# Two-layer attention and feed-forward kernel: the expert stage written out chunk by chunk in place of a loop over three chunks

## The chip, the cores and the metric

The kernel runs on one core of a Trainium2 chip. The metric is the device time of one execution in microseconds (us). The engines are TensorE (PE; its weight loads are shown apart as PEld), VectorE (DVE), ScalarE (ACT), GpSimd (POOL) and SyncE (SP, which here only issues DMA transfers). Each engine has its own stream of instructions, and the streams meet at semaphores.

## What is computed

Two layers work on 128 sequences of 64 tokens with 128 features. Each adds an attention over a context and a feed-forward part to the running x. The change touches only the feed-forward part of the first layer, a mixture of 64 experts (eight chosen for each token) and one shared expert:

```python
def _L0_ffn_ref(x, centroids, expert_biases, Ws_up, Ws_down, W_up, W_down):
    ...
    shared = jax.nn.silu(xf @ Ws_up) @ Ws_down
    aff = xf @ centroids.T
    biased = aff + expert_biases
    _, idx = jax.lax.top_k(biased, TOP_K)
    sel = jnp.take_along_axis(aff, idx, axis=1)
    w = jax.nn.sigmoid(sel)
    w = w / (jnp.sum(w, axis=-1, keepdims=True) + 1e-08)
    cw = jnp.zeros((T, E), dtype=x.dtype).at[jnp.arange(T)[:, None], idx].add(w)
    h = jax.nn.silu(jnp.einsum('td,edf->etf', xf, W_up))
    y = jnp.einsum('etf,efd->etd', h, W_down)
    routed = jnp.einsum('etd,te->td', y, cw)
    return (shared + routed).reshape(B, S, D)
...
    x = x + _L0_xattn_ref(_layernorm(x, axis=-1), ctx_1024, ctx_1024, ...)
    x = x + _L0_ffn_ref(_layernorm(x, axis=-1), ...)
    x = x + _L1_xattn_ref(_layernorm(x, axis=-1), ctx_1024, ctx_1024, ...)
    x = x + _L1_ffn_ref(_layernorm(x, axis=-1), ...)
```

## The kernel before

The kernel has four stages, each a block in which every engine has its own code and at whose end all engines meet: `attention`, `experts`, `tail` (second attention) and `ternary` (second feed-forward part). The change is inside `experts`, which takes the time from 320.9 us to some 1102 us of the profiled execution.

`experts` computes all 64 experts for all tokens and weighs each expert's result with a gate that is zero where the token did not choose it. The tokens come in 16 chunks of 512. The experts come in pairs, and the pairs in groups of two, so that a chunk has 17 turns: 16 full ones, and turn 16 (`FULL`) with the shared expert alone. A turn n goes through the engines in this order:

- PE, `up` (L1133 to L1135): three matmuls for each pair (the weights and the tokens are split in a high and a low part) into the buffer `pu`.
- ACT (L1099): SiLU in place. DVE (L1036): product with the gates, `m`. The gates come by DMA from `scratch` in memory (L994, issued by SP).
- ACT (L1109), one turn later: the high part `mh` of `m`. The low part `ml` is made by DVE (L1041) or, for the turns 4, 5, 7, 10, 14 and for 16 in half size, by POOL (L955, L952).
- PE, `down` (L1144, L1145, L1148), three turns later: the sum over experts in `py`. For turn 0 of a chunk it first waits until ACT has copied out the `py` of the chunk before (`y_copy`, L1086), which ACT does in turn 2.

Beside this each chunk has work that is tied to fixed turns i: the layer norm and the routing of the next chunks (in `ChunkNorm` and `Routing`), and the adding of the finished chunk to x. Three of these places matter here. In turn 10, DVE sums a chunk's eight gates (`add_up`, L805), adds the epsilon (`add_eps`, L809, four numbers for each partition) and inverts (L813); POOL's L955 for turn 10 comes at nearly the same time. In turns 11 and 12, DVE takes the statistics of chunk c + 2 (L638, L644). In turn 12, POOL waits for them and normalises (`norm`, L650 to L657), and behind that in POOL's queue stands L955 for turn 14, whose `ml` PE needs in turn 0 of the next chunk.

The order is written out by hand in one function `step(n, r, chunk)` for each engine. `drive` (L905) calls it for each turn: for chunk 0 with plain numbers; then in a hardware loop (`eng.Fori`, L911) whose body is three chunks long and runs four times, for chunks 1 to 12; then with plain numbers again for chunks 13 to 15. Three chunks are a period, because the rings of three buffers come round. In the loop body a turn's number is only known in a register, so the values that semaphores are waited for, and the places in x, are worked out by register instructions (L52, and L638 for the addresses). `wait_apart` (L55) also adds an instruction that counts up an idle semaphore where the value is in a register; with plain numbers it is a bare wait. `live`, `exists` and `first` leave out work at either end.

Of the kernel before, what the change touches and what calls it, by code (L numbers as in the profile page):

```python
# [54 lines left out]
def wait_apart(eng, sem, value, idle):  # L55

    at_least(eng, sem, value)
    if not isinstance(value, int):
        eng.sem_inc(idle, 1)
# [16 lines left out]
def live(t, lag, count):  # L76

    return not isinstance(t, int) or 0 <= t - lag < count
# [757 lines left out]
def experts(nc, cst, x_res, norms, routing, entry, y_mean, y_rstd, sem, chunks=TILES // 4):  # L836
# [7 lines left out]
    GROUPS = (PAIRS + 1) // 2  # L844
    FULL = GROUPS - 1
    turns = chunks * GROUPS
    looped = (chunks - 4) // 3 * 3
    RING = 3
    SPREAD = 4
    with ExitStack() as mem:  # L850
# [51 lines left out]
            else:  # L902
                at_least(eng, gated, c * FULL + i + 1)

        def drive(eng, step):  # L905

            for n in range(GROUPS):
                step(n, n, lambda lag, n=n: (n - lag) // GROUPS)  # L910
            with eng.Fori(0, looped // 3) as g:  # L911
                for r in range(3 * GROUPS):
                    step(g * (3 * GROUPS) + (GROUPS + r), GROUPS + r, lambda lag, g=g, r=r: g * 3 + (1 + (r - lag) // GROUPS))
            for n in range((1 + looped) * GROUPS, turns + RING):
                step(n, n % (3 * GROUPS), lambda lag, n=n: (n - lag) // GROUPS)

        def exists(c):
# [5 lines left out]
        with nc.Block() as block:  # L923
            @block.gpsimd
            def _(pool):
                pool.sem_inc(y_rooted, 2)

                def after(semaphore, value):
                    wait_apart(pool, semaphore, value, idle["pool"])

                def y_root(c):

                    after(y_stats, 2 * c + 2)
                    nc.gpsimd.tensor_scalar(y_ve[:], y_mv[:, :, 1:2], 1e-5, None, ALU.add).then_inc(y_eps, 1)
                    nc.gpsimd.tensor_tensor(y_mean[:, bass.ds(c * 4, 4)], y_mv[:, :, 0], cst["ones"][:, 0:4],
                                            ALU.mult).then_inc(y_rooted, 1)
                    after(y_eps, c + 1)
                    nc.gpsimd.tensor_tensor(y_rstd[:, bass.ds(c * 4, 4)], y_ve[:, :, 0], cst["mhalf"][:].to_broadcast([P, 4]),
                                            ALU.pow).then_inc(y_rooted, 1)

                def norm(c):
                    routing.await_turned(pool, c - 1)
                    norms.norm(pool, x_res, cst["mhalf"], c, idle["pool"])

                def step(n, r, chunk):
                    i = r % GROUPS
                    if live(n, 1, turns) and (r - 1) % GROUPS in low_by_pool:
                        k = (r - 1) % 3
                        after(m_high, n)
                        after(down_done, n - 3)  # L950
                        if (r - 1) % GROUPS == FULL:
                            nc.gpsimd.tensor_tensor(ml[k][:, 0, :], m[k][:, 0, :], mh[k][:, 0, :].bitcast(F32),  # L952
                                                    ALU.subtract).then_inc(m_low[1], 1)
                        else:
                            nc.gpsimd.tensor_tensor(flat(ml[k][:]), flat(m[k][:]), flat(mh[k][:]).bitcast(F32),  # L955
                                                    ALU.subtract).then_inc(m_low[1], 1)
                    if not live(n, 0, turns):
                        return
                    c, first = chunk(0), isinstance(n, int) and n < GROUPS
                    if exists(c + 1):  # L960
                        if i == 1:
                            routing.low_part(pool, c + 1, (r // GROUPS + 1) % 3)
                        if i == 2:
                            routing.ends(pool, nc.gpsimd, "pool", c + 1)
                        if i == 3:
                            routing.fourth_powers(pool, nc.gpsimd, "pool", c + 1)
                        if i == 4:
                            routing.denominator(pool, nc.gpsimd, "pool", c + 1)
                        if i == 9:
                            routing.weights(pool, nc.gpsimd, "pool", c + 1)  # L970
                        if i == 11:
                            routing.gates_of(pool, nc.gpsimd, "pool", c + 1)
                    if i == 9 and not first:
                        y_root(c - 1)
                    if i == 12 and exists(c + 2):
                        norm(c + 2)
                drive(pool, step)

            @block.sync
            def _(sp):  # L980
                def step(n, r, chunk):
                    if not live(n, 0, turns):
                        return
                    i, c = r % GROUPS, chunk(0)
                    if i == FULL:
                        if exists(c + 1):
                            routing.store(sp, c + 1, (r // GROUPS + 1) % 3)
                        return
                    if i == 0:
                        wait_apart(sp, stored, 16 * (c + 1), idle["sp"])  # L990
                    wait_apart(sp, gated, c * FULL + (i + 1 - SPREAD), idle["sp"])
                    rows = scratch[(r // GROUPS) % 3, 4 * i:4 * i + 4].rearrange("(j e) t -> e j t", e=2)
                    for e in range(2):
                        sp.dma_start(gt[i % SPREAD][64 * e:64 * e + 64], rows[e].unsqueeze(0).to_broadcast([FH, 2, 512])).then_inc(  # L994
                            spread[i % SPREAD], 16)
                drive(sp, step)
                for n in range(4):
                    entry.load(sp, n)
                sp.wait_ge(stored, 16 * chunks)

            @block.vector
            def _(dve):
# [25 lines left out]
                def step(n, r, chunk):  # L1028
# [43 lines left out]
                    if exists(c + 2):  # L1072
                        if i == 11:
                            stats_of(c + 2)
                        if i == 12:
                            aggregate(c + 2)
                drive(dve, step)
                dve.wait_ge(y_rooted, 4)
                for n in range(2):
                    entry.norm_in(x_res, y_mean, y_rstd, n)  # L1080
# [1 line left out]
            @block.scalar  # L1082
            def _(act):
                def y_copy(c):
                    at_least(act, down_done, (c + 1) * GROUPS)
                    nc.scalar.copy(yT, py[:]).then_inc(y_out, 1)  # L1086

                def step(n, r, chunk):
                    i, k = r % GROUPS, r % 3
                    first = isinstance(n, int) and n < GROUPS  # L1090
                    if live(n, 0, turns):
                        c = chunk(0)
                        at_least(act, up_done, n + 1)
                        if i == FULL:
                            if live(n, RING, turns + RING):
                                await_low(act, (r - RING) % GROUPS, chunk(RING))
                            nc.scalar.activation(m[k][:, 0, :], pu[k][:, 0, :], ACT.Silu).then_inc(silued, 1)
                        else:
                            nc.scalar.activation(flat(pu[k][:]), flat(pu[k][:]), ACT.Silu).then_inc(silued, 1)  # L1099
                        if i == 2 and not first:  # L1100
                            y_copy(c - 1)
                    if live(n, 1, turns):
                        k, before = (r - 1) % 3, (r - 1) % GROUPS
                        await_gated(act, before, chunk(1))
                        at_least(act, down_done, n - 3)
                        if before == FULL:
                            nc.scalar.copy(mh[k][:, 0, :], m[k][:, 0, :]).then_inc(m_high, 1)
                        else:
                            nc.scalar.copy(flat(mh[k][:]), flat(m[k][:])).then_inc(m_high, 1)  # L1109
                    if not live(n, 0, turns) or not exists(c + 1):  # L1110
                        return
                    if i == 0:
                        routing.turned_copy(act, pt, c + 1)
                        routing.high_part(act, pt, (r // GROUPS + 1) % 3)
                    if i == 2:
                        routing.affinities_out(act, pt_aff, c + 1)
                    if i == 13:
                        routing.gates_copy(act, pt, c + 1)
                drive(act, step)
                y_copy(chunks - 1)  # L1120

            @block.tensor
            def _(pe):
# [27 lines left out]
                def step(n, r, chunk):  # L1151
# [20 lines left out]
                    if i == 13 and exists(c + 1):  # L1172
                        wait_apart(pe, y_added, c, idle["pe"])
                        routing.turn_gates(pe, pt, c + 1)
                drive(pe, step)


def dft_tables():
# [611 lines left out]
```

## Time and profile before

| | us |
|---|---|
| median of 3 runs | 1292.41 (1291.2 to 1294.64) |
| the profiled execution | 1289.56 |
| its span, first to last instruction | 1287.8 |
| PE busy | 1238.5 (96%) |
| DVE busy | 1067.4 (83%) |
| ACT busy | 922.9 (72%) |
| POOL busy | 770.2 (60%) |

The span is what the trace covers; 1.8 us of the profiled execution lie outside it. Times in the trace count from the start of the span. Each row below is from this one execution.

### The profile page before, as it was taken

To read this page: it belongs to the slowest core of one execution; us is meant where nothing else is said; L and a number is where in the kernel's file an instruction comes from. 1 tells how busy PE (TensorE), PEld (TensorE's weight loads), DVE (VectorE), ACT (ScalarE), POOL (GpSimd) and SP (SyncE) were. 2 spreads that over 40 slices of the span, in tenths; PEclk is the share of its full clock that TensorE was granted. 3 is DMA by queue.
4 is the path that set the end of the run, shared out by engine and by line. 5 is a ranking of instruction groups with operands and counts; after the bars stand their busy time and mean duration, and the time that the engine had idled before them with its cause. 6 is when DMAs were issued, how large, how long until landed. Compare 5 with 4: busy or idle time off the path is not lost. (4 is left out here: it accounts for less than half of the span.)

```text
span 1287.8 us, 29796 instructions
## 1 busy us (share of the span) xinstructions
PE 1238.5 (96%) x9113; PEld 997.9 (77%) x9113; DVE 1067.4 (83%) x2062; ACT 922.9 (72%) x1525; POOL 770.2 (60%) x828
## 2 busy tenths in 40 slices
PE   6999999996999999999999999999999999899986
PEld 4777777774788888788878878788888888799976
DVE  5878888886788879879889889879889887689986
ACT  4778888884777777676777777777777776777761
POOL 3765665662556556656657556656657533477773
PEclk9999999998999999999999999999999999999988
DMA  5401101100976776876876877876777777111004
GB/s 127 111 27 32 30 29 31 30 20 5 218 179 167 184 181 154 194 169 152 195 168 168 194 171 164 194 170 163 183 172 178 182 183 181 34 34 30 22 2 131
DMA packets 126149, 159.56 MB, mean 124 GB/s; under 512 B 20840, under 2 KB 59504, under 8 KB 126064
## 3 DMA queue, kind: packets, MB, share of 16 engines
q1 hardware_dynamic: 120750, 156.06, 50.3%
q10 hardware_dynamic: 5314, 2.53, 0.7%
q8 instruction: 34, 0.56, 0.2%
q14 instruction: 51, 0.42, 0.1%
HBM read 152.25 MB, written 6.29 MB: 123 GB/s over the span
## 5 line engine op out<-in xcount | busy, mean ns | idle before, releaser
L1036 DVE TENSOR_TENSOR e_m<-e_pu,raw 128x1024 f32<-128x1024 f32 x256 | 309.7, 1211 | 93.2 <-ACT e_pu L1099 67.7
L1099 ACT ACTIVATE e_pu<-e_pu 128x1024 f32<-128x1024 f32 x256 | 258.6, 1010 | 161.8 <-PE e_pu L1135 160.4
L1109 ACT CAST e_mh<-e_m 128x1024 fp32r<-128x1024 f32 x256 | 267.9, 1047 | 44.7 <-DVE e_m L1036 40.3
L955 POOL TENSOR_TENSOR e_ml<-e_m,e_mh 128x1024 fp32r<-128x1024 f32 x80 | 193.1, 2417 | 125.1 <-ACT e_mh L1109 124.9
L1041 DVE TENSOR_TENSOR e_ml<-e_m,e_mh 128x1024 fp32r<-128x1024 f32 x176 | 238.7, 1356 | 21.6 <-ACT e_mh L1109 20.6
L1133 PE MATMUL e_pu<-r_xh,wuh 128*128 128x512 f32 x528 | 215.0, 407 | 1.9 <-PEq L208 1.9
L1144 PE MATMUL e_py<-e_mh,wdh 128*128 128x512 f32 x528 | 208.5, 395 | 2.1 <-ACT held L1086 2.1
L1135 PE MATMUL e_pu<-r_xl,wuh 128*128 128x512 f32 x528 | 209.4, 397 | 0.0
L1134 PE MATMUL e_pu<-r_xh,wul 128*128 128x512 f32 x528 | 209.3, 396 | 0.0
L1145 PE MATMUL e_py<-e_mh,wdl 128*128 128x512 f32 x528 | 209.0, 396 | 0.0
L1148 PE MATMUL e_py<-e_ml,wdh 128*128 128x512 f32 x528 | 168.2, 397 | 1.1 <-DVE e_ml L1041 0.6
L1148 PEld LDWEIGHTS e_py<-e_ml,wdh 128*128 128x128 f32 x528 | 98.1, 188 | 28.8 <-POOL e_ml L955 4.0
L1144 PEld LDWEIGHTS e_py<-e_mh,wdh 128*128 128x128 f32 x528 | 99.1, 188 | 26.9 <-issue 3.3
L1133 PEld LDWEIGHTS e_pu<-r_xh,wuh 128*128 128x128 f32 x528 | 99.8, 189 | 24.1 <-issue 2.5
L1135 PEld LDWEIGHTS e_pu<-r_xl,wuh 128*128 128x128 f32 x528 | 99.7, 189 | 24.2
L1145 PEld LDWEIGHTS e_py<-e_mh,wdl 128*128 128x128 f32 x528 | 99.1, 188 | 24.3
L1134 PEld LDWEIGHTS e_pu<-r_xh,wul 128*128 128x128 f32 x528 | 100.0, 189 | 21.2
L377 POOL TENSOR_TENSOR kx<-qkT,hmask 128x512 f32<-128x512 f32 x64 | 66.6, 1041 | 80.4 <-ACT qkT L479 78.6
L267 DVE TENSOR_REDUCE mx<-ps 128x16 f32<-128x1024 f32 x64 | 78.3, 1224 | 42.6 <-PE ps L530 42.6
L569 PEld LDWEIGHTS pob<-vx,pT 128*64 128x64 f32 x2048 | 65.1, 138 | 26.8 <-issue 20.4
L272 DVE TENSOR_TENSOR prob<-ps,mx 128x1024 f32<-128x1024 f32 x64 | 77.6, 1212 | 0.1
L569 PE MATMUL pob<-vx,pT 128*64 128x18 f32 x2048 | 71.3, 212 | 1.8 <-ACT vx L488 0.5
(231 smaller groups left out, 2360.6 us busy)
## 6 DMA issues: line engine op xcount, KB each, us to landing
raw<-gates_scratch SPq DMA_DIRECT2D x512, 256.0 KB, 4.3
x_res<-in_x_dram SPq DMA_DIRECT2D x64, 64.0 KB, 1.8
xcT<-in_ctxT_dram SPq DMA_DIRECT2D x64, 64.0 KB, 1.9
held<-in_ctx_dram SPq DMA_DIRECT2D x32, 128.0 KB, 2.2
raw<-in_L_ffn_W_up_dram SPq DMA_DIRECT2D x4, 512.0 KB, 4.4
raw<-in_L_ffn_W_down_dram SPq DMA_DIRECT2D x4, 512.0 KB, 6.0
gates_scratch<-raw SPq DMA_DIRECT2D x16, 128.0 KB, 2.3
out_dram<-t_res SPq DMA_DIRECT2D x8, 256.0 KB, 2.9
```

Of the source, the lines that this page charges most:

```text
L569: ins = nc.tensor.matmul(po[q, 2 * j:2 * j + 2, :], pT[:, r % 2, j, q], vx[:, r % 4, j, b], start=True, stop=True)
L955: nc.gpsimd.tensor_tensor(flat(ml[k][:]), flat(m[k][:]), flat(mh[k][:]).bitcast(F32), ALU.subtract).then_inc(m_low[1], 1)
L1036: nc.vector.tensor_tensor(flat(m[r % 3][:]), flat(pu[r % 3][:]), flat(gt[i % SPREAD]), ALU.mult).then_inc(gated, 1)
L1041: nc.vector.tensor_tensor(flat(ml[k][:]), flat(m[k][:]), flat(mh[k][:]).bitcast(F32), ALU.subtract).then_inc(m_low[0], 1)
L1099: nc.scalar.activation(flat(pu[k][:]), flat(pu[k][:]), ACT.Silu).then_inc(silued, 1)
L1109: nc.scalar.copy(flat(mh[k][:]), flat(m[k][:])).then_inc(m_high, 1)
L1133: nc.tensor.matmul(pu[k][:, j, :], cst["wuh"][:, w], xh[:, b, :], start=True, stop=False)
L1134: nc.tensor.matmul(pu[k][:, j, :], cst["wul"][:, w], xh[:, b, :], start=False, stop=False)
L1135: ins = nc.tensor.matmul(pu[k][:, j, :], cst["wuh"][:, w], xl[:, b, :], start=False, stop=True)
L1144: nc.tensor.matmul(py[:], cst["wdh"][:, w], mh[k][:, j, :], start=(i == 0 and j == 0), stop=False)
L1145: nc.tensor.matmul(py[:], cst["wdl"][:, w], mh[k][:, j, :], start=False, stop=False)
L1148: ins = nc.tensor.matmul(py[:], cst["wdh"][:, w], ml[k][:, j, :], start=False, stop=(i == FULL))
```

## The change

The loop is taken out. `drive` calls `step` with plain numbers for all 16 chunks, and no longer takes the engine. Nothing else in the file changes; lines behind it move up by up to eight.

```diff
-    looped = (chunks - 4) // 3 * 3
...
-        def drive(eng, step):
...
-            for n in range(GROUPS):
-                step(n, n, lambda lag, n=n: (n - lag) // GROUPS)
-            with eng.Fori(0, looped // 3) as g:
-                for r in range(3 * GROUPS):
-                    step(g * (3 * GROUPS) + (GROUPS + r), GROUPS + r, lambda lag, g=g, r=r: g * 3 + (1 + (r - lag) // GROUPS))
-            for n in range((1 + looped) * GROUPS, turns + RING):
+        def drive(step):
+
+            for n in range(turns + RING):
                 step(n, n % (3 * GROUPS), lambda lag, n=n: (n - lag) // GROUPS)
...
-                drive(pool, step)
+                drive(step)
```

The last line stands five times, once for each engine. What each engine executes of matmuls, vector work and transfers, and in which order, is as before; what goes is register instructions, branches and counts of idle semaphores.

The first place is DVE's stream where chunk 3 ends (turn 16 and the end of the loop's body). Before:

```order
L52 REGISTER_ALU
L52 REGISTER_ALU [waits e_silu]
L1036 TENSOR_TENSOR e_m<-e_pu,raw 128x1024 [waits e_spread3,e_m_low_dve]
L1041 TENSOR_TENSOR e_ml<-e_m,e_mh 128x1024 [waits e_down,e_m_high]
L911 REGISTER_ALU
L911 COMPARE_AND_BRANCH
L1036 TENSOR_TENSOR e_m<-e_pu,raw 128x1024 [waits e_spread0,e_m_low_pool,e_silu]
```

Now (L1028 and L1033 are L1036 and L1041 of before):

```order
L1033 TENSOR_TENSOR e_ml<-e_m,e_mh 128x1024 [waits e_down,e_m_high]
L1028 TENSOR_TENSOR e_m<-e_pu,raw 128x1024 [waits e_spread3,e_m_low_dve,e_silu]
L1033 TENSOR_TENSOR e_ml<-e_m,e_mh 128x1024 [waits e_down,e_m_high]
L1028 TENSOR_TENSOR e_m<-e_pu,raw 128x1024 [waits e_spread0,e_m_low_pool,e_silu]
L1028 TENSOR_TENSOR e_m<-e_pu,raw 128x1024 [waits e_spread1,e_m_low_dve,e_silu]
```

The compare and branch stood between the last work of one chunk and the first of the next, and the row behind it belongs to chunk 13 and is reached only when the loop ends; now the next chunk's first product stands there.

The second place is DVE's stream in turn 10, where the gates are summed. Before, in the loop's body:

```order
L1041 TENSOR_TENSOR e_ml<-e_m,e_mh 128x1024 [waits e_down,e_m_high]
L52 REGISTER_ALU
L805 TENSOR_REDUCE raw<-raw 128x4 [waits r_weighed]
L809 TENSOR_SCALAR raw<-raw 128x4 [waits r_added_up]
L813 RECIPROCAL raw<-raw 128x4 [waits r_added_up]
L52 REGISTER_ALU
L52 REGISTER_ALU [waits e_silu]
L1036 TENSOR_TENSOR e_m<-e_pu,raw 128x1024 [waits e_spread3,e_m_low_dve]
```

Now:

```order
L1033 TENSOR_TENSOR e_ml<-e_m,e_mh 128x1024 [waits e_down,e_m_high]
L805 TENSOR_REDUCE raw<-raw 128x4 [waits r_weighed]
L809 TENSOR_SCALAR raw<-raw 128x4 [waits r_added_up]
L813 RECIPROCAL raw<-raw 128x4 [waits r_added_up]
L1028 TENSOR_TENSOR e_m<-e_pu,raw 128x1024 [waits e_spread3,e_m_low_dve,e_silu]
```

The five operations are the same in the same order; the register instructions between them are gone.

## Rows read from the trace of the kernel before

**Rows 1.** Page, busy time of an engine, share of the span, instructions.
```profile
PE 1238.5 (96%) x9113; PEld 997.9 (77%) x9113; DVE 1067.4 (83%) x2062; ACT 922.9 (72%) x1525; POOL 770.2 (60%) x828
```

**Rows 2.** Stretches: start:end, length, PE busy (instructions), clock, DMA share, GB/s.
```profile
368.74:1003.43 634.69, 632.12 (x2836) 1.00 0.74 176
513.92:564.16 50.24, 49.18 (x220) 1.00 0.75 178
564.16:612.57 48.41, 48.41 (x219) 1.00 0.69 168
612.57:661.35 48.78, 48.67 (x220) 1.00 0.73 174
661.35:710.92 49.57, 48.92 (x220) 1.00 0.75 182
759.33:808.07 48.74, 48.67 (x219) 1.00 0.78 175
808.07:857.53 49.46, 48.91 (x219) 1.00 0.78 181
905.95:954.70 48.75, 48.67 (x220) 1.00 0.75 175
954.70:1003.43 48.73, 48.68 (x220) 1.00 0.80 184
1003.43:1051.83 48.40, 48.40 (x220) 1.00 0.73 177
```

**Rows 3.** Waits from 368.74 to 1103: engine, line, releaser, total, times, longest.
```profile
DVE e_m L1036 <- issue: 12.5, 3, 4.7
...
PEld e_py L1148 <- POOL e_ml L955: 4.0, 8, 0.5
...
PE e_py L1144 <- ACT held L1086: 2.1, 3, 1.0
```

**Rows 4.** L911's branches (min/median/max ns, first and last start), and timeline around 514.
```profile
L911 DVEq COMPARE_BRANCH  x4: 55/62/74, 515.5 to 956.3; - x4
...
515.39 2.09 DVE L1041 TENSOR_TENSOR e_ml<-e_m,e_mh 128x1024 fp32r<-128x1024 f32 x1 [1.11 <-ACT e_mh L1109]
522.16 2.35 DVE L1036 TENSOR_TENSOR e_m<-e_pu,raw 128x1024 f32<-128x1024 f32 x2 [4.67 <-issue]
...
525.38 0.58 ACT L1086 COPY held<-e_py 128x512 f32<-128x512 f32 x1
...
526.11 0.47 PE L1144 MATMUL e_py<-e_mh,wdh 128*128 128x512 f32 x1 [1.00 <-ACT held L1086]
```

**Rows 5.** Timeline of PE, DVE and POOL: start, us, work [idle before].
```profile
566.49 0.63 PE L1148 MATMUL e_py<-e_ml,wdh 128*128 128x512 f32 x2
...
600.21 2.17 DVE L809 TENSOR_SCALAR raw<-raw 128x4 f32<-128x4 f32 x1 [0.15 <-DVE raw L805]
...
599.95 2.40 POOL L955 TENSOR_TENSOR e_ml<-e_m,e_mh 128x1024 fp32r<-128x1024 f32 x1 [1.13 <-ACT e_mh L1109]
...
612.72 2.40 POOL L955 TENSOR_TENSOR e_ml<-e_m,e_mh 128x1024 fp32r<-128x1024 f32 x1
...
990.46 0.17 DVE L809 TENSOR_SCALAR raw<-raw 128x4 f32<-128x4 f32 x1
...
355.87 2.39 DVE L809 TENSOR_SCALAR raw<-raw 128x4 f32<-128x4 f32 x1
...
368.33 2.40 POOL L955 TENSOR_TENSOR e_ml<-e_m,e_mh 128x1024 fp32r<-128x1024 f32 x1
```

**Rows 6.** DMA queues that carry instructions: packets, MB; 320.90:513.92, then 513.92:954.70, then 954.70:1101.62.
```profile
q8 instruction: 7, 0.11, 0.3%
...
q14 instruction: 18, 0.15, 0.1%
...
q8 instruction: 6, 0.10, 0.3%
```

More of the change, by code:

```diff
@@ L995, in step @@
                             spread[i % SPREAD], 16)
-                drive(sp, step)
+                drive(step)
                 for n in range(4):
@@ L1076, in step @@
                             aggregate(c + 2)
-                drive(dve, step)
+                drive(step)
                 dve.wait_ge(y_rooted, 4)
@@ L1118, in step @@
                         routing.gates_copy(act, pt, c + 1)
-                drive(act, step)
+                drive(step)
                 y_copy(chunks - 1)
@@ L1174, in step @@
                         routing.turn_gates(pe, pt, c + 1)
-                drive(pe, step)
+                drive(step)
 def dft_tables():
```

## The prediction, made before the changed kernel ran

> **What bounds the kernel now.** The page comes first: PE is busy for 96% of the span [rows 1]. In such a kernel an edit is worth what it does to PE's waits, and nothing else. The next view is the stretches by chunk, cut where PE starts each chunk's first `up` matmul [rows 2]. Written out, chunk 14 takes 48.40 us and PE is busy for all of it, at the full granted clock; so does chunk 5, which is inside the loop, with 48.41. A chunk therefore costs PE 48.40 us whether its code is in the loop or not, although in the loop every engine also runs register instructions. They run beside the work and cost PE nothing by themselves. What differs are some of the chunks: 4, 7 and 10 (50.24, 49.57, 49.46), and 6, 9, 12 and 13 (48.78, 48.74, 48.75, 48.73). The chunks 1, 2, 3, 8 and 11 that aren't shown lie at the floor, since they are what is left in the sum of the stretch below.
>
> The waits name three causes [rows 3]: DVE's product stood still three times for "issue", 12.5 us in all; PE's first `down` waited three times for ACT's copy of `py`, 2.1 us; PE's weight load for `down` waited eight times for POOL's low part, 4.0 us.
>
> **The loop's way back.** Chunks 4, 7 and 10 are those that follow a taken branch. The timeline shows how it gets to PE [rows 4]. DVE's branch takes 0.06 us, but after its last work in chunk 3, which ends at 517.48, DVE does nothing until 522.16, with no semaphore to blame: 4.67 us. The product comes late, ACT stands behind it in its own queue, copies `py` out only at 525.38, and PE's `down` of turn 0 starts at 526.11 after 1.00 us idle. Since PE runs three turns ahead, 4.67 us on DVE become about 1.5 on PE. The queues that carry instructions show what happens [rows 6]. The smaller pieces (q14) keep coming, 18 in the three passes from 513.92 to 954.70. In q8 there are seven in the first 193 us and six in the last 147, and none in between: one engine with big pieces (PE, as it has by far the most instructions) has its loop body at hand, and others must fetch theirs again after each branch. The Trainium skill, in "Runtime: NRT & Kernel Launch", section Instruction fetch mechanics, says that straight code is fetched ahead, and that a taken branch to a place outside the window must wait for a fetch. By that rule alone the gain would be the three ways back, 3.0 us (worked out below), and written-out code would cost nothing. The trace agrees that far: the branch stands four times, and the fourth time, where it isn't taken, leaves no such wait.
>
> **The waits for POOL.** Chunks 6, 9, 12 and 13 lose 0.33 to 0.38 us each in turn 0, where PE waits for POOL's low part of turn 14. The wait is counted eight times, so chunks 4, 7 and 10 have it as well (the eighth is in the last chunk); I take the mean of the four, 0.35, for these too. POOL is late because its normalising is late, that because DVE's statistics are, and those because of one small instruction in turn 10 [rows 5]. In chunk 5 DVE's L809 starts at 600.21, 0.26 us after POOL's L955, and takes 2.17 us for four numbers a partition: it ends when POOL's ends (599.95 + 2.40 = 602.35). In chunk 13, written out, it starts at 990.46 and takes 0.17. So whoever is first goes, and DVE loses 2.0 us when it is second. The Trainium skill has this in "SBUF — State Buffer": the port pair that DVE and GpSimd share is an exclusive lock, and the one that issues second is blocked until the first is done. By it the outcome hangs on the order of two starts, as the rows show.
>
> What does the change do there? Without the register instructions L809 comes earlier against L955. In chunk 13 it won. In chunk 0, also written out, it lost (355.87, 2.39 us), and even so POOL's low part of turn 14 ran from 368.33 to 370.73, while PE, which began chunk 1 at 368.74, needs it after ten matmuls. That took 2.33 us in chunk 5, where nothing was late (564.16 to 566.49), so it is at 371.07 here: POOL was 0.34 us early. In chunk 5 of the loop, also lost, POOL's ran from 612.72 to 615.12, against a need at 612.57 + 2.33 = 614.90: late. Written out, then, PE doesn't wait for it in either outcome. I take zero for this wait.
>
> **The sum.** From the start of chunk 1 to the end of chunk 13 the kernel takes 634.69 us. Thirteen chunks at 48.40 are 629.20. The difference is 5.49 us. Of it the chunks 4, 7 and 10 hold 1.84 + 1.17 + 1.06 = 4.07 (3 x 0.35 = 1.05 of which is the wait for POOL, so that the ways back are 3.02), and 6, 9, 12 and 13 hold 0.38 + 0.34 + 0.35 + 0.33 = 1.40. Chunks 0, 14 and 15 and the other stages have the same code as before, and I take zero for them. After a stall is gone nothing else is late next, since PE is at its floor: more can't be won.
>
> What is added is code to fetch. Seven written-out chunks (0, 13, 14, 15, and 1 to 3 on their first pass through the body) had 7 + 6 = 13 of the large pieces [rows 6]; nine more chunks need about nine sevenths of 13, or 17 more. Their price, from the nearest rows: chunk 14 fetched its share with the DMA engines busy for 0.73 of the time, and took 48.40 with PE busy throughout, so zero. The other end of the bound is a wait as after the branch, 1.5 us on PE each. Below zero it can't be. I take zero, because it is the same sort of fetch in the same traffic. The code of the later stages moves in memory, so a fetch at the entry of a block may come sooner or later; for that I allow 1 us either way.
>
> The profiled execution would go from 1289.56 to 1284.1 (its span from 1287.8 to 1282.3). It lies 2.85 us below the median of the runs, so from the median: 1292.41 - 5.49 = **1286.9 us**, 0.42% less.
>
> **The rivals.** (a) *The waits for POOL stay.* The tie between L809 and L955 is close, and POOL may be late at chunk starts although it wasn't in the written-out ones. If they stay where they are now, seven times 0.35, the gain is 5.49 - 2.45 = 3.04 us: 1289.4. If they come at every one of the fifteen starts, 5.25 us are lost and the gain is 0.2 us: 1292.2. For it: the wait came at seven of the thirteen starts in question, and the margin in chunk 0 is 0.34 us. Against it: no start behind a written-out chunk has it. It decides when POOL's low part ends over 2.33 us after the chunk starts.
>
> (b) *Slower by code fetches.* The place is PE's own stream. In three of four passes it fetched nothing, and now it streams from memory beside 170 to 180 GB/s of gates. If a piece isn't there in time, PE itself stands. Seventeen at 1.5 us are 25.5 us less 5.5 gained: 1312. It costs more than the change gives from 0.32 us a piece on. Against it: none of the 13 pieces in written-out chunks left a mark.
>
> (c) *Only part of the way back goes*, since DVE, ACT and POOL still fetch their small pieces and one could come late in a full queue. Half of the 3.02 us of the ways back gives 1.5 less gained: 1288.4.
>
> (d) *It does nothing that can be seen.* If the 4.67 us on DVE came from something that recurs every three chunks, a buffer or a gate transfer, and not from the branch, only the waits for POOL go: 1292.41 - 2.45 = 1290.0. Against it: the straight chunks 13 and 14 come three and four after chunk 10 and have no such wait.
>
> **How the numbers follow.** Chances: my forecast (a gain of 4.5 to 6.5 us) 0.66; (a) 0.15; (b) 0.05; (c) 0.09; (d) 0.05. About 0.3%, or 3.9 us, is what a measurement of this kernel can tell from no change. My forecast counts for faster; of (a) and (c), 0.24 together, 0.08 lie above that line, most of it from (c), which is on it: faster 0.74. The rest of (a) and (c), and (d), give same 0.21, and (b) slower 0.05. The runs of before spread over 3.4 us, so 1.7 either way is added to a median. The range goes from 1286.9 - 1 - 1.7, or 1284.0, to the first form of (a) with 1.7 on top, 1291.0; outside lie (b) and the second form of (a).
>
> **What would show each step.** In the stretches by chunk: 48.40 for chunks 1 to 13, with PE busy throughout, confirms the sum; 49.5 or 50 at chunks 4, 7 and 10 refutes the branch as cause. In the waits: "issue" at DVE's product gone, PE's wait for ACT's copy gone, PEld's wait for POOL gone (if it stays, it is (a)). L809 at 0.17 us in chunks 1 to 14 if DVE wins the tie, 2.2 to 2.4 where not, and in that case still no wait on PE. In the queues: about 17 more pieces in q8, at even distances. PE idle for "issue" inside a chunk would be (b). The experts' stage should be 5.5 us shorter and the others as before.

## The result and the profile after

The changed kernel takes 1283.65 us (median of 4 runs, 1282.73 to 1285.07), against 1292.36 us before (4 runs): a ratio of 0.9931, with a 95% interval of 0.9914 to 0.9949. It is faster, as forecast, but by 8.7 us on these medians where 5.5 were forecast, and the time lies 0.35 us below the predicted range. A second comparison with more runs (below) gives a smaller gain, a ratio of 0.995.

The profiled execution took 1285.07 us, with a span of 1283.3. Its page answers to [rows 1]:

```profile
PE 1237.0 (96%) x9113; PEld 999.1 (78%) x9113; DVE 1058.2 (82%) x2062; ACT 920.6 (72%) x1525; POOL 764.7 (60%) x828
```

The counts of work are the same. The stretches by chunk answer to [rows 2] (start:end, length, PE busy with its instructions, clock, DMA share, GB/s). The first row is chunks 1 to 13, the others are chunks 1, 4 and 13:

```profile
369.95:999.08 629.13, 629.13 (x2836) 1.00 0.75 177
369.95:418.35 48.40, 48.40 (x219) 1.00 0.78 184
515.15:563.54 48.39, 48.39 (x219) 1.00 0.73 177
950.69:999.08 48.39, 48.39 (x220) 1.00 0.75 176
```

634.69 us became 629.13, with PE busy for all of it; the prediction had 629.20. Of the waits in [rows 3] two are gone and the third is down to one, in the last chunk. That is all there is of these kinds from chunk 1 to the end of the stage:

```profile
PEld e_py L1140 <- POOL e_ml L947: 0.5, 1, 0.5
```

L809 takes 0.17 us but for chunk 0, where it takes 2.40. It wins narrowly: in most chunks it starts 0.04 us ahead of POOL's L947, where in the loop it had started 0.25 us behind L955 whenever it lost. Its row of the view by line (count, min/median/max ns):

```profile
L809 DVE TENSOR_SCALAR raw<-raw x16: 169/170/2400, 318.6 to 1034.5; 128x4 f32<-128x4 f32 x16
```

Pieces of code on the DMA queues in chunks 1 to 13: the large ones (q8) come in the loop's former place too, 22 where there had been 7, and leave no mark.

```profile
q8 instruction: 22, 0.36, 0.3%
q14 instruction: 23, 0.19, 0.1%
```

Where the span's 4.5 us come from is seen when it is cut at the start of the experts' first matmul and at their last. After:

```profile
0.00:322.47 322.47, 296.45 (x4383) 0.96 0.17 44
322.47:1097.73 775.26, 774.23 (x3467) 1.00 0.75 177
1097.73:1283.30 185.57, 166.34 (x1264) 0.95 0.15 44
```

Before, the same view:

```profile
0.00:320.90 320.90, 294.19 (x4383) 0.97 0.17 44
320.90:1102.09 781.19, 777.95 (x3468) 1.00 0.74 176
1102.09:1287.80 185.71, 166.38 (x1264) 0.95 0.15 44
```

The experts give 5.93 us (5.56 of it in chunks 1 to 13), and the later stages 0.14. The attention stage, whose code is the same, took 1.57 us longer in this one execution, and had lost them before its 30th us. So one profile of each kernel says 4.5, and the medians say 8.7; the sum for chunks 1 to 13 is met within 0.1 us. The experiments had to show which of the numbers is the change.

### The profile page after: what moved, and what is told of

Its sections match the earlier page's. It is cut to its first block and busy times, and to the rows that moved or that the text cites. A ratio compares the mean times of both kernels' runs of the same rounds, so it can differ in the third digit from the quotient of the medians.

```text
span 1283.3 us, 27099 instructions
## 1 busy us (share of the span) xinstructions
PE 1237.0 (96%) x9113; PEld 999.1 (78%) x9113; DVE 1058.2 (82%) x2062; ACT 920.6 (72%) x1525; POOL 764.7 (60%) x828
## 5 line engine op out<-in xcount | busy, mean ns | idle before, releaser
L1028 DVE TENSOR_TENSOR e_m<-e_pu,raw 128x1024 f32<-128x1024 f32 x256 | 309.9, 1211 | 95.0 <-ACT e_pu L1091 84.0
L947 POOL TENSOR_TENSOR e_ml<-e_m,e_mh 128x1024 fp32r<-128x1024 f32 x80 | 192.3, 2405 | 142.5 <-ACT e_mh L1101 141.0
L1033 DVE TENSOR_TENSOR e_ml<-e_m,e_mh 128x1024 fp32r<-128x1024 f32 x176 | 240.5, 1366 | 25.4 <-ACT e_mh L1101 25.4
```

The lines of the kernel that those rows point to most:

```text
L1028: nc.vector.tensor_tensor(flat(m[r % 3][:]), flat(pu[r % 3][:]), flat(gt[i % SPREAD]), ALU.mult).then_inc(gated, 1)
L1033: nc.vector.tensor_tensor(flat(ml[k][:]), flat(m[k][:]), flat(mh[k][:]).bitcast(F32), ALU.subtract).then_inc(m_low[0], 1)
```

## The experiments

All are compared with the kernel before on the same chip. "Faster by" is the difference of the medians.

### The two kernels again

No edit. First the kernel before:

> The kernel of before, unchanged, for a second profile and the spread of its executions. Theory A (the gain is the 5.5 us of the experts' stage, and what the medians show beyond it, 8.7 us in all, is how executions of one program differ at the start): chunks 1 to 13 again take 634 to 636 us, the three chunks behind a taken branch again 49.4 to 50.3, and the spans differ by 1 to 3 us outside the experts' stage. Theory B (the ways back cost more in most executions than in the profiled one): chunks 1 to 13 take 636 to 639 us here.

1291.94 us (12 runs, 1290.22 to 1294.38). Its profile has, in the view of [rows 2], chunks 1 to 13, then chunks 4, 5, 7 and 10:

```profile
368.81:1006.04 637.23, 632.64 (x2835) 1.00 0.74 175
514.00:564.86 50.86, 49.17 (x219) 1.00 0.76 176
564.86:613.30 48.44, 48.44 (x219) 1.00 0.69 167
...
662.05:712.71 50.66, 49.15 (x219) 1.00 0.78 177
809.90:860.15 50.25, 49.18 (x220) 1.00 0.78 177
```

The same program now loses 637.23 - 629.13 = 8.10 us in these chunks, where the first profile had lost 5.56. The difference is in chunks 4, 7 and 10, which are 2.47, 2.27 and 1.86 us over 48.39, where [rows 2] had 1.85, 1.18 and 1.07. Of the three waits the first grew most (12.5 us in [rows 3]):

```profile
DVE e_m L1036 <- issue: 15.0, 3, 5.3
PEld e_py L1148 <- POOL e_ml L955: 4.1, 8, 0.5
PE e_py L1144 <- ACT held L1086: 3.0, 3, 1.0
```

The stop behind the branch is longer in one execution than in another. How much of it reaches PE is seen when DVE's three stops are set beside the three chunks. The two of the first profile that [rows 4] doesn't show, then the three of this one:

```profile
668.90 1.22 DVE L1036 TENSOR_TENSOR e_m<-e_pu,raw 128x1024 f32<-128x1024 f32 x1 [4.00 <-issue]
815.52 2.36 DVE L1036 TENSOR_TENSOR e_m<-e_pu,raw 128x1024 f32<-128x1024 f32 x2 [3.86 <-issue]
...
522.85 2.36 DVE L1036 TENSOR_TENSOR e_m<-e_pu,raw 128x1024 f32<-128x1024 f32 x2 [5.26 <-issue]
670.70 2.35 DVE L1036 TENSOR_TENSOR e_m<-e_pu,raw 128x1024 f32<-128x1024 f32 x2 [5.07 <-issue]
818.13 2.35 DVE L1036 TENSOR_TENSOR e_m<-e_pu,raw 128x1024 f32<-128x1024 f32 x2 [4.66 <-issue]
```

Stops of 4.67, 4.00 and 3.86 us cost 1.85, 1.18 and 1.07 us; stops of 5.26, 5.07 and 4.66 cost 2.47, 2.27 and 1.86. The difference is 2.8 us all six times. So a fixed 2.8 us of each stop is taken up, since PE works ahead of DVE, and every further microsecond costs PE a whole one. The loss therefore varies far more than the stop: 20% more stop (12.5 to 15.0 us) made 61% more loss in these three chunks (4.10 to 6.60 us).

Chunks 1 to 13 were expected at 634 to 636 by theory A and at 636 to 639 by theory B; 637.23 is B's.

> The changed kernel, unchanged. Both theories: chunks 1 to 14 at 48.39 to 48.41 us again. Theory A: against the kernel before, the ratio of the medians comes nearer to 0.9957, a gain of 5.5 us. Theory B: it stays at 0.993, a gain of 8 to 9 us.

1284.98 us (6 runs) against 1291.73 (23 runs): ratio 0.995, interval 0.9937 to 0.9962, faster by 6.75 us. That is between the two theories: B was right on the ways back in the second profile, and the first 8.7 us were of four runs a side. The kernel before ran from 1289.02 to 1294.33 here; the changed one from 1283.16 to 1285.53. The two widths can't be compared as they stand, 23 runs against 6; more on the spread below.

### How often the branch is taken

```diff
-    looped = (chunks - 4) // 3 * 3
+    looped = 3
```

> The loop runs once (chunks 1 to 3 in its body, the branch never taken), 4 to 15 written out. If the taken branch costs the time: no stop of VectorE for issue, no chunk above 48.8, and the only loss is 0.3 us at the start of chunk 4, behind a lost L809 in chunk 3; 0.3 us over the changed kernel. If the loop costs by being entered and left, or if it is the period of three chunks: a stop at chunk 4 as before, 1.5 us or more over the changed kernel.

1284.9 us, faster by 6.83 (ratio 0.9949, 0.9933 to 0.9965), the time of the changed kernel. The branch is there and isn't taken. Not even the 0.3 us at chunk 4 came; but a loop of one pass left none of L52's register instructions in the experts' stage, so this run doesn't test them; it shows that the loop whose branch isn't taken cost nothing that can be told here.

```diff
-    looped = (chunks - 4) // 3 * 3
+    looped = 6
```

> The loop runs twice (chunks 1 to 6), 7 to 15 written out: one taken branch, before chunk 4. If the cost goes with the taken branches: chunk 4 at 50 to 51, and 0.35 each at the starts of chunks 6 and 7: 2.3 to 3.2 us over the changed kernel, and executions that differ by 2.5 to 3.5 us instead of 5. If with the loop's being there: 6 us over the changed kernel, as before.

1287.07 us, 5.3 less than before (ratio 0.9961, 0.9944 to 0.9977) and 2.4 to 2.7 more than two written-out kernels on the same chip (`a_late2` and `all_out`, below). Chunks 1 to 13, then 4, 6, 7 and 8:

```profile
370.73:1002.55 631.82, 630.48 (x2836) 1.00 0.75 177
515.90:566.27 50.37, 49.18 (x219) 1.00 0.77 177
614.71:663.47 48.76, 48.66 (x220) 1.00 0.75 175
663.47:712.19 48.72, 48.67 (x220) 1.00 0.80 185
712.19:760.58 48.39, 48.39 (x220) 1.00 0.74 177
```

One taken branch, one chunk of the dear sort (a stop of 4.76 us on DVE and a loss of 1.98, again 2.8 apart); the late low parts stand at the starts of 6 and 7 and no more behind that. The cost goes with the taken branches, and rival (d) with its period of three chunks is out.

### Which engine's branch it is

`drive` was given a list of engines for which it writes the code out, so that the loop could be kept for some alone. The main lines of the edit (each call also gets its engine's name):

```diff
+        written = ("dve",)
...
-        def drive(eng, step):
+        def drive(eng, step, name):
+            if name in written:
+                for n in range(turns + RING):
+                    step(n, n % (3 * GROUPS), lambda lag, n=n: (n - lag) // GROUPS)
+                return
```

> The kernel of before, with VectorE's stream alone written out; TensorE, ScalarE, GpSimd and SyncE keep the loop of three chunks. If VectorE's fetch behind the branch is the whole way back, and its register instructions the cause of the lost L809: all chunks from 1 to 14 at 48.4 us, no wait for GpSimd at their starts, and 6.5 us faster than before, as the changed kernel. If each engine's branch costs its own part (their fetches are in a row on the same queue, at 3.4, 7.5 and 12.9 us behind the branch): 0.3 us or more remain at each of the chunks 4, 7 and 10, 1 to 3 us over the changed kernel.

1284.15 us, faster by 8.2 (ratio 0.9934, 0.9921 to 0.9946): all that the change brings, with DVE's stream alone. Chunks 1 to 13:

```profile
369.05:998.19 629.14, 629.14 (x2836) 1.00 0.74 177
```

The reverse has `written = ("act", "pool", "sp", "pe")`:

> The reverse: VectorE alone keeps the loop, the others are written out. If VectorE is the whole cause: chunks 4, 7 and 10 at 49.2 to 50.5 us as before. For the starts of the other chunks: L809 is lost in seven chunks or more, since VectorE is late and GpSimd is not; TensorE waits for GpSimd's low part there by 0.1 to 0.3 us, less than before because GpSimd has no register instructions. Within 2 us of before. If the others' branches matter: 2 us or more faster than before.

1293.95 us, not faster at all, rather 1.6 us slower (ratio 1.0012, 1.0002 to 1.0022). Chunks 1 to 13, then 4, 7 and 10:

```profile
367.80:1004.73 636.93, 631.48 (x2835) 1.00 0.74 175
513.14:563.91 50.77, 49.02 (x219) 1.00 0.74 175
660.77:711.68 50.91, 49.00 (x220) 1.00 0.72 168
808.57:859.38 50.81, 49.01 (x220) 1.00 0.73 169
```

Two of its waits (L1042 and L1154 are L1036 and L1148 here):

```profile
DVE e_m L1042 <- issue: 16.6, 3, 5.6
...
PEld e_py L1154 <- POOL e_ml L961: 2.3, 9, 0.3
```

DVE is the whole cause: its three stops are even longer here than in either profile of before, and why isn't known. PE's waits for POOL at the starts of chunks are there as well, and smaller (0.3 us at the most, 0.5 before), as was expected of a POOL without register instructions; no run tests that reason by itself.

### Is it the size of the loop's body

Counted in the trace of the kernel before, from one branch to the next, the body of three chunks has 451 instructions on DVE, 287 on ACT, 218 on POOL, 206 on SP and 1485 on PE (matmuls and weight loads counted apart), within one. In `dve_out` the last four loop, take all three branches, and PE loses nothing by it. `act_grown` is `dve_out` with ACT's body made as large as DVE's, by counts on a semaphore that nobody waits for:

```diff
+                def grown(n, r, chunk):
+                    step(n, r, chunk)
+                    if not isinstance(n, int):
+                        for k in range(4):
+                            act.sem_inc(idle["act"], 1)
-                drive(act, step, "act")
+                drive(act, grown, "act")
```

> VectorE written out, the others in the loop of three chunks (which had no way back that cost anything), and ScalarE's loop body grown from 287 to 491 instructions by four semaphore counts a turn that nobody waits for. If a body above some size between 287 and 451 must be fetched again at each taken branch: small code pieces come after each of the three branches, ScalarE stands for 3 to 6 us for issue, chunks 4, 7 and 10 cost 1 to 4 us more each, 3 to 9 us in all over the same kernel without the counts; chunks 5, 6, 8, 9 stay at 48.4. If the way back is something of VectorE's own, or of work rather than of code: no stop, 1284 to 1285.

1289.23 us (12 runs), 3.1 less than before (ratio 0.9976, 0.9964 to 0.9988) and 5.1 more than `dve_out`. That one ran on another chip, but the kernel before took 1292.31 us there and 1292.35 here. Chunks 1 to 13, then 4, 7, 10 and 5:

```profile
370.02:1003.65 633.63, 629.97 (x2835) 1.00 0.73 176
515.19:565.24 50.05, 48.66 (x219) 1.00 0.71 171
662.03:711.98 49.95, 48.68 (x220) 1.00 0.70 172
808.78:858.46 49.68, 48.69 (x220) 1.00 0.69 172
565.24:613.63 48.39, 48.39 (x219) 1.00 0.75 177
```

ACT's timeline around its first branch, at 514.6 us:

```profile
514.57 1.04 ACT L1115 CAST e_mh<-e_m 128x1024 fp32r<-128x1024 f32 x1
520.22 1.01 ACT L1105 ACTIVATE e_pu<-e_pu 128x1024 f32<-128x1024 f32 x1 [4.61 <-PE e_pu L1146]
```

PE's wait for it:

```profile
PE e_pt L746 <- ACT r_xh L736: 3.7, 3, 1.4
```

ACT now stands for 4.61 us behind the branch, where it stood for 1.18 us in `dve_out`, and PE waits for it three times. (The timeline puts the end of this stop and of the second, 4.49 us, down to PE's matmul; the third, of 4.21 us, stands as "issue". What they share is the place behind the branch.) The three chunks lose 1.66, 1.56 and 1.29 us, each 2.9 us less than ACT's stop: again a fixed part is taken up and the rest is lost whole. The chunks in between are at 48.39, so the counts cost nothing by themselves: it is the size of the body. Small pieces of code: 33 from chunk 1 to 13, where `dve_out` had 16. By their times in the trace, two come 3 to 8 us behind each of ACT's three taken branches; `dve_out` has none in the 20 us behind any of the three. This is the direct sign that code is fetched there. Which size between 287 and 451 is the limit wasn't measured.

The same for PE, with a body of six chunks (2967 instructions on PE, 884 on DVE, 571 on ACT from branch to branch), in the kernel before:

```diff
-            with eng.Fori(0, looped // 3) as g:
-                for r in range(3 * GROUPS):
+            with eng.Fori(0, looped // 6) as g:
+                for r in range(6 * GROUPS):
```

(and 6 for 3 in the step's arguments.)

> The loop's body is six chunks, run twice: one taken branch, before chunk 7, but register instructions in all of chunks 1 to 12. If VectorE's fetch behind the branch is all there is: chunk 7 costs 1.0 to 1.8 us more, chunk 4 nothing of that sort; about 1.5 us for the way back and 0.35 for each late low part of GpSimd. If TensorE has a body of three chunks at hand and one of six does not fit: its queue of large code pieces goes on in the second pass (about 12 pieces, none in the kernel before), and TensorE itself stands at the branch for 2 to 5 us, since its fetch can't be hidden. If it fits: no large piece in the second pass.

1294.55 us, slower than before by 2.8 (ratio 1.0024, 1.0015 to 1.0033), although two of three ways back are gone. PE's branches (min/median/max ns):

```profile
L911 PEldq COMPARE_BRANCH  x2: 83/2401/4719, 660.6 to 957.8; - x2
```

Its wait behind them:

```profile
PE e_pu L1133 <- issue: 4.2, 1, 4.2
```

Chunks 6 and 7:

```profile
612.47:665.58 53.11, 48.83 (x219) 1.00 0.71 174
665.58:715.48 49.90, 49.90 (x218) 0.97 0.67 167
```

The taken branch alone took 4.72 us on PE and nothing hides that, as PE is the bound; 1.5 us more went in the next chunk, where the granted clock was at its half level for a part (0.97 on the mean). In the second pass 12 of the large pieces came, where [rows 6] had none in any pass but the first.

### The small instruction in turn 10

`b_no_eps` is the kernel before with `add_eps` left out in the experts' stage; the reciprocal inverts the bare sum. The kernel leaves out the 1e-8 of the reference.

> The kernel of before with L809 left out of the experts' stage (the 1e-8 added to each sum of gates; the output moves by rounding), so that no operation of VectorE stands against GpSimd's L955 at that place. If the lost L809 makes GpSimd late: the waits for its low part at the starts of 4, 6, 7, 9, 10, 12 and 13 go, 7 times 0.3 to 0.35, 2.2 to 2.5 us faster than before; chunks 6, 9, 12 and 13 at 48.4. If it is GpSimd's own load in the loop (its register instructions) that makes it late: they stay, and the time is that of before.

1288.65 us, faster by 3.7 (ratio 0.9974, 0.9962 to 0.9986). Chunks 1 to 13, then 4, 7, 10 and 6:

```profile
368.02:1000.19 632.17, 629.96 (x2836) 1.00 0.73 176
513.22:562.91 49.69, 48.69 (x219) 1.00 0.73 172
659.70:709.35 49.65, 48.65 (x219) 1.00 0.71 173
806.14:854.99 48.85, 48.64 (x219) 1.00 0.74 175
611.31:659.70 48.39, 48.39 (x220) 1.00 0.72 176
```

Chunk 6, and 13 likewise, is at the floor with the loop and all its other register instructions there: the lost L809 made POOL late, and nothing else did. The ways back stay, but they cost less: stops of 5.21, 5.17 and 4.36 us lose 1.30, 1.26 and 0.46, so 3.9 us of each are taken up here instead of 2.8. Without the 2 us lost at L809, DVE is earlier: its last work before the first stop ends 2.5 us after PE has begun chunk 4, and in the kernel before 3.6 us after. In chunks 4, 7 and 10 the lost L809 was thus worth 1.1 us each at equal stops, and not 0.35. With the other four chunks that makes 4.7 us where 2.2 to 2.5 were expected; the measured 3.7 lies between, and its interval (1.8 to 4.9) holds both.

This run also prices the ways back in medians. The profiled execution, 1285.62 us, is the shortest of its seven, and loses 632.17 - 629.13 = 3.04 us; by the median `b_no_eps` takes 4.5 us more than `dve_out` on the same chip (1288.65 against 1284.15; with 7 and 6 runs this is good to about 1.5 us).

Does the changed kernel live on winning that tie? `a_late` is the changed kernel with one small reciprocal, its result unused, ahead of L809:

> The changed kernel with one small reciprocal (0.18 us, its result unused) in front of L809, so that L809 starts behind GpSimd's L955 in every chunk and is blocked for 2.2 us. By the prediction's margin of 0.34 us in chunk 0: GpSimd's low part is still in time, TensorE waits nowhere, the time is that of the changed kernel, chunks at 48.4. By the rival, the changed kernel lives on winning the tie: 0.1 to 0.35 us lost at each chunk's start, 1.5 to 5 us slower than the changed kernel.

1284.68 us, 7.6 less than before (ratio 0.9935, 0.9919 to 0.9952). This run answered the question by halves: the delay was too small, and L809 was blocked for 2.3 us in six of fifteen chunks and took 0.14 us in the others, while PE waited in none of them. So it was done again with two larger ones:

```diff
+                            for k in range(2):
+                                nc.vector.reciprocal(routing.pad[:, k], cst["ones"][:, 0:E])
                             routing.add_eps(dve, c + 1)
```

> The changed kernel with two small reciprocals of 64 columns in front of L809, some 0.6 to 0.9 us, so that L809 is clearly behind GpSimd's L947 and blocked until it ends. By the prediction's margin: TensorE still waits nowhere, chunks at 48.4, the time of the changed kernel. By the rival, that the changed kernel lives on winning this tie: 0.1 to 0.35 us lost at the start of each of 14 chunks, 1.5 to 5 us slower.

1284.69 us (ratio 0.9941, 0.9922 to 0.9959), the time of the changed kernel. L809 (L810 here) is blocked until POOL's operation ends (timeline):

```profile
598.97 1.71 DVE L810 TENSOR_SCALAR raw<-raw 128x4 f32<-128x4 f32 x1
```

POOL then waits for DVE, in fourteen chunks:

```profile
POOL raw L818 <- DVE raw L814: 4.4, 14, 0.3
```

PE loses nothing (its weight load waits once, for 0.2 us, and no matmul stands for it); chunks 1 to 13:

```profile
369.19:998.32 629.13, 629.13 (x2836) 1.00 0.75 177
```

### A version that goes further

`all_out` writes out the attention stage's loop as well; its body is four tiles and runs twelve times. From branch to branch it has 80 instructions on DVE, 65 on ACT, 48 on POOL, 38 on SP and 574 on PE. Two conditions that told the loop's turns by their registers are put in numbers too; they aren't shown.

```diff
-    first = -(-lag // unroll) * unroll
-    for t in range(first):
-        step(t, t % unroll)
-    with eng.Fori(first // unroll, count // unroll) as g:
-        for r in range(unroll):
-            step(g * unroll + r, r)
-    for t in range(count, count + lag):
+    for t in range(count + lag):
         step(t, t % unroll)
```

> The changed kernel with the attention stage's loop of four tiles (12 passes, 11 taken branches) written out too. That loop's bodies are small, and no code piece is fetched between its branches except in TensorE's queue at its start, so by the theory its way back costs next to nothing: TensorE's branch of 0.22 us eleven times at the most, 0 to 2.4 us faster than the changed kernel, most likely under 1. If every taken branch cost what those of the experts' stage do: 5 us or more faster. If straight code costs fetches where a small body costs none: slower by 1 us or more.

1284.42 us (6 runs; ratio 0.9934, 0.9919 to 0.995): nothing over the changed kernel that these runs can tell. The first stage took 321.51 us, between the 320.90 and 322.47 of the two first profiles. Eleven taken branches with small bodies cost nothing that shows here.

## Why the prediction was right, and where it was wrong

**Right: what bounds the kernel, and the floor.** 48.40 us a chunk for thirteen chunks was forecast as 629.20 us, and 629.13 measured, with PE busy throughout. What the profile was to show, it showed: no stop for issue, no wait for ACT's copy, no wait at the chunk starts, 15 more large pieces of code (17 were worked out) with no stall.

**Right: the way back is a fetch of code, on DVE.** The prediction said "others must fetch theirs again". `dve_out` and `dve_in` sharpen it: of the five engines DVE alone. That it is a fetch, and goes with the size of the body, is shown by `act_grown`. The claim that PE has its body at hand was right, and `six_body` shows what it would have cost otherwise.

**Right: the waits for POOL,** by `b_no_eps`, and also that in written-out code PE waits in neither outcome of the tie, by `a_late2`. The margin of 0.34 us read in chunk 0 was enough in all fourteen chunks. The way of telling it was too simple: "whoever is first goes" holds to some hundredths of a microsecond only. In `a_late` L810 started 0.04 us behind POOL's operation and still took 0.14 us, while in chunk 0 of the kernel before 0.02 us behind was too late.

**Wrong: the size of the ways back, and so the range.** The step that failed is the term "the ways back are 3.02". It was read from one execution and applied to a median. In that execution DVE stopped for 12.5 us in all; in the second profile it was 15.0, and the three chunks lost 2.47 + 2.27 + 1.86 - 1.05 = 5.55 us instead of 3.0. With 5.55 + 2.45 the gain is 8.0 us, and the forecast from the same median would have been 1284.4. That profile was of an execution 1.3 us above its median, so 5.55 is rather too much, as 3.02 was too little. What should have raised the question stood in the text: the profiled execution was 2.85 us below the median of the runs, and below the shortest of them (1291.2). The prediction took this for an offset to be added again ("1292.41 - 5.49"), though an execution may be shorter than the others because just these stalls were short in it.

"4.67 us on DVE become about 1.5 on PE" was true of that one stop and hid the rule: a fixed part is taken up and the rest counts in full. By it small differences between stops are large ones in the loss. The split of the sum was wrong too: 0.35 us in each of the chunks 4, 7 and 10 was put down to the wait for POOL, but with the lost L809 gone these chunks lose 1.1 us less at equal stops (`b_no_eps`). As the change removes both, this did not touch the forecast.

**How large the gain is.** Seven sets of runs are of kernels that keep PE busy without a stop in chunks 1 to 13: `after` and `a_again` (the changed kernel), `one_pass`, `dve_out`, `a_late`, `a_late2` and `all_out`. Against before they gain 8.7, 6.75, 6.8, 8.2, 7.6, 7.7 and 7.9 us. Their 34 runs on all chips have a median of 1284.42 us, and the 59 runs of before beside the experiments one of 1292.02: 7.6 us. Less the 2.45 us that the sum gives the waits for POOL, some 5.1 are left, by the prediction's own split, for the term that was put at 3.02. The 1283.65 us of the first comparison is itself 0.8 us below that median, so part of the miss was the chance of four runs. A slip in the sum made no difference: 1286.9 - 1 - 1.7 is 1284.2, not 1284.0, and 1283.65 lies below both.

**The spread.** The prediction added the spread of the runs either way, as noise. Part of it was stall, which the change removes. But only part: the standard deviation is 1.57 us over the 59 runs of before and still 1.17 us over the 34 without the stalls. What makes the rest vary wasn't studied; the one difference seen is 1.57 us in the first 30 us of the attention stage.

**The rivals.** (a), the waits for POOL stay: out, by the profile after and by `a_late2`. (b), slower by code fetches: out, 22 large pieces without a wait. (c), part of the way back stays: out, by 48.39 us in chunk 4 and no stop for issue in the profile after, with 23 small pieces fetched. (d), something with a period of three chunks: out, by `two_pass`.

## What to carry to other kernels

In this kernel a hardware loop cost nothing as long as its body stayed at hand on every engine. Look for a wait put down to "issue" behind the branch, and for small pieces of code on the DMA queues just after it; find the one engine that has it, and write out that engine's code alone. (A body made shorter should do as well, but no run tried it.) A longer body is no remedy: it can move the fetch to the engine that is the bound. Where a stall on one engine is partly hidden by another's lead, set several stops beside the losses: the hidden part may be a fixed time, not a share. And before a gain is read off one profiled execution, compare its time with the other runs: where it is shorter than they are, the stalls to be removed may be short in it too.

## What the runs showed of the hardware

- A loop body of 451 instructions on DVE, or of 491 on ACT, was fetched again after each taken branch; bodies of 287 on ACT, 218 on POOL, 206 on SP and 1485 on PE were not, and one of 2967 on PE was. The stops were 3.9 to 5.6 us on DVE, 4.2 to 4.6 on ACT and 4.7 on PE.
- The same stops varied from one execution to the next: 12.5 and 15.0 us in all in two executions of one program.
- A loop's branch that isn't taken left no stop (the last pass of the kernel before, and `one_pass`).
- A stop of 4.7 us on PE was followed by a stretch of half the granted clock, and the chunk with it took 1.5 us more (`six_body`).
- Of two operations of DVE and POOL that start within some hundredths of a microsecond, the order of the records doesn't tell which is blocked.
